# Attention scores with the queries held still: 128 masked query columns, 64 keys passing, four PSUM banks

## The chip, the cores and the metric
The kernel runs on one core of a Trainium2 chip. The metric is the device time of one execution in microseconds. Before the change three runs gave 1270.83, 1270.95 and 1271.89 us, a median of 1270.95 us.

## The reference
Input x has shape (4, 64, 128, 128). Two residual blocks follow each other:
- x is normalised over its 64 channels and cut into windows of 8 x 8 = 64 tokens. q, k and v come from three 64 x 64 projections; there are 4 heads of 16 channels. Each head has scores q k^T / 4 plus a relative position bias (64 x 64 per head), a softmax over the 64 keys, and the product with v. An output projection and the residual x follow.
- Each token is normalised over its channels. A router takes the two best of 8 experts, and their 64 x 64 products are mixed by the renormalised probabilities and added to the token.

All of it is float32 (gates travel as split bfloat16).

## The kernel before
**Tiling.** A strip is 8 rows of one image, 16 windows; there are 16 strips in each of 4 images, 64 in all. On 128 partitions the two halves of the strip lie above each other (`b` = 0 or 1 is the half, in the code also `ab`), so 8 windows lie side by side in two groups `n` of four units `i`; units 0 and 1 are "pair 0", units 2 and 3 "pair 1".

**Stages and slots.** `pipeline` runs slots j = -1 to 66. In slot j a strip is in each of five stages: j+1 is projected and its pair 0 gets scores, j is attended (pair 1, softmax, turning the probabilities), j-1 is put out, j-2 is routed, j-3 is mixed by the experts. Each engine has its order inside a slot written out by hand in its own function `slot`: PE at L533, ACT at L719, DVE at L994, POOL at L1145, SP (which issues all DMAs) at L321. The engines are held together by counting semaphores alone; an engine that waits holds up all that stands behind it in its order. In 24 of the slots (8 for each of images 1 to 3, n = 4 to 11 in `planned`, L242) DVE also sums squares of the next image, `sum_squares` at L815; in 24 (n = 3 to 10) PE also turns input planes, `take` at L352.

**What the change touches.**
- `project` (L365) multiplies the normalised strip by the weights: keys and values first, then, later in the slot, the queries (L571). ACT copies them out of `B_S`: `copy_k` twice (L653; copy e keeps only the heads of parity e by a mask and zeroes the others), `copy_v`, and later `copy_q` once (L648).
- `scores` (L397) makes the scores of one pair: 16 matmuls (2 units, 2 groups n, 2 halves b, 2 head pairs hp), each with 32 contracted rows, a stationary operand of 64 query columns and a moving operand of 128 masked key columns (two head parities by 64 keys). A float32 matmul leaves two matmul and two weight-load records, so a group of scores is 32 records. They lie on four row tiles by two column tiles of the array and all write the two banks of `B_S`. Pair 1 of strip j is the first thing in PE's slot j, pair 0 of strip j+1 comes in the middle (L579).
- `bias` (L878, DVE) adds the position bias and writes `prob` in SBUF; `maxima` (L885, DVE), `shift` (L1117, POOL), `exps` (L673, ACT) and `turn_probs` (L414, PE) follow.
- Between them on DVE stand the gates of the experts: `gate` (L987) for u = 0, 1, 3, 5, 7, and `routing` (L924), small steps in the bank `B_E`. DVE's order in the middle of a slot is: gate 0, gate 1, sum_squares (where there is one), routing steps 1 to 8, gate 3, normalise, bias of pair 0, maxima, gate 5, add_input, gate 7, token_mean.
- PE's order over the same stretch is: expert_biases (L508), gates 0 and 1 (L518), logits, gates 2, turn_logits, gates 3, project queries, experts 0 (L530), turn_probs 2, gates 4, scores of pair 0, take, experts 1, gates 6, turn_probs 3, gates 5, project_out, turn_values, gates 7, experts 2 and 3.

PSUM has eight banks: two for `B_S`, one each for `B_T` (turning), `B_O` (attention output, later its projection), `B_E` (router), `B_P` (sums of probabilities, later odd gates), `B_G` (even gates), `B_Y` (result).

Of the kernel before, what the change touches and what calls it, by code (L numbers as in the profile page):

```python
# [74 lines left out]
def build(nc, x, wqkv, qkvb, kmask, kbias, wproj, wrout, brout, wexp, bexp, bmask, relb, ident, sel, rank, bproj, out):  # L75
    ctx = ExitStack()
    with ctx:
# [3 lines left out]
        def sem(name, per=1, primed=0):  # L81
# [9 lines left out]
        q_bias = sb("q_bias", [P, 1])  # L91
        k_mask = sb("k_mask", [P, 2])
        k_bias = sb("k_bias", [P, 2])
# [9 lines left out]
        rel = sb("rel", [P, HEADS * 2 * NTOK])  # L103
# [18 lines left out]
        q_t = sb("q_t", [P, 2, PAIRS, NTOK])  # L122
        k_m = sb("k_m", [P, 2, PAIRS, 2, NTOK])
# [3 lines left out]
        prob = sb("prob", [P, UNITS, HEADS, 2, NTOK])  # L127
        mx = sb("mx", [P, UNITS, 2 * HEADS])
# [26 lines left out]
        FIRST_SQ = (x_sq, prob[:, 0:2].rearrange("p i h n k -> p (i h n k)").rearrange("p (m c h) -> p m c h", m=2, c=4))  # L155
        B_S = ctx.enter_context(nc.psum_tensor("bank_s", [P, 2, BANK], F32))
        B_T, B_O, B_E, B_P, B_G, B_Y = (
            ctx.enter_context(nc.psum_tensor(f"bank_{n}", [P, BANK], F32)) for n in "toepgy")
        S_S = B_S[:, :, :].rearrange("p g (i e n k) -> p g i e n k", i=2, e=2, n=2)
# [26 lines left out]
        q_ready = sem("q_ready")  # L186
        k_ready = sem("k_ready", 2)
# [47 lines left out]
        consts = [(w_qkv, wqkv), (b_qkv, qkvb), (k_mask, kmask), (k_bias, kbias), (w_proj, wproj), (w_rout, wrout),  # L235
# [112 lines left out]
        def _(pe):  # L348
# [48 lines left out]
            def scores(g, p, pair):  # L397

                if pair == 0:
                    pe.wait_ge(q_ready.sem, q_ready.at(g, 1))  # L400
                    pe.wait_ge(k_ready.sem, k_ready.at(g, 2))
                if not (isinstance(g, int) and g == 0 and pair == 0):
                    pe.wait_ge(s_biased.sem, s_biased.at(g, pair))
                for i in range(2):
                    for n in range(2):
                        for b in range(2):
                            for hp in range(2):
                                rows = slice(C * b + 2 * DH * hp, C * b + 2 * DH * hp + 2 * DH)
                                w = UNITS * n + 2 * pair + i
                                last = mm(S_S[C * b:C * b + C, hp, i, :, n, :], q_t[rows, p, w, :], k_m[rows, p, w, :, :],  # L410
# [3 lines left out]
            def turn_probs(g, i, work):  # L414
# [9 lines left out]
                for h in range(HEADS):  # L424
                    last = tr(B_T[:, h * P:(h + 1) * P], prob[:, i, h].rearrange("p n k -> p (n k)"), idn[:, :])  # L425
                last.then_inc(pt_done.sem, 1)

            def values(g, p):

                pe.wait_ge(pt_ready.sem, pt_ready.at(g, 4))  # L430
                pe.wait_ge(vbd_ready.sem, vbd_ready.at(g, 2))
                pe.wait_ge(x2_ready.sem, x2_ready.at(g))
                for i in range(UNITS):
                    for b in range(2):
                        at = (UNITS * b + i) * NTOK
                        for h in range(HEADS):
                            rows = slice(2 * DH * h, 2 * DH * h + 2 * DH)
                            last = mm(B_O[rows, at:at + NTOK], v_bd[:, p, i, b, h, :],  # L438
                                      prob_t[:, p, i, h, b * NTOK:(b + 1) * NTOK], start=True, stop=True,
# [3 lines left out]
            def prob_sums(g, p):  # L443
# [6 lines left out]
                for i in range(UNITS):  # L450
                    for h in range(HEADS):
                        rows = slice(2 * DH * h, 2 * DH * h + 2 * DH)
                        dst = B_P[rows, :].rearrange("p (b i q) -> p b i q", b=2, i=UNITS)[:, :, i, :]
                        last = mm(dst, ones_bd[:, :], prob_t[:, p, i, h, :].rearrange("p (b q) -> p b q", b=2),  # L454
# [34 lines left out]
            def turn_gates(g):  # L489
                pe.wait_ge(route.sem, route.at(g, route.per))  # L490
                pe.sem_inc(passed, 1)
# [18 lines left out]
            def gates(g, u):  # L510

                if u == 1:
# [20 lines left out]
            def slot(j, p, work, on):  # L533
# [3 lines left out]
                if attending:  # L537
                    scores(j, p, 1)
# [4 lines left out]
                if projecting:  # L543
                    project(j + 1, KEYS_VALUES)
                if outputting:
                    values(j - 1, 1 - p)
                if mixing:
                    residual(j - 3, 1 - p)
                    turn_gates(j - 3)
# [20 lines left out]
                if projecting:  # L570
                    project(j + 1, QUERIES)  # L571
# [6 lines left out]
                if projecting:  # L578
                    scores(j + 1, 1 - p, 0)  # L579
# [8 lines left out]
                if mixing:  # L588
                    gates(j - 3, 5)
# [21 lines left out]
        def _(act):  # L611
# [28 lines left out]
            def first_root(batch):  # L640
# [4 lines left out]
                A(q_bias[:, :], b_qkv[:, 0:1], ACT.Copy, scale=float(DH) ** -0.5).then_inc(set_act.sem, 1)  # L645
                act.wait_ge(set_act.sem, 2)

            def copy_q(g, p):  # L648
# [609 lines left out]
```

## Time and profile before

| | before |
|---|---|
| median of three runs | 1270.95 us |
| profiled execution | 1268.81 us |
| its span, first to last instruction | 1267.0 us |
| PE busy | 1192.4 us, 94% |
| DVE busy | 1053.9 us, 83% |
| ACT busy | 920.4 us, 73% |
| POOL busy | 1081.7 us, 85% |
| mean granted TensorE clock | 0.983 of full speed |

Engines: PE is TensorE's matmuls, PEld its weight loads (they overlap PE), DVE VectorE, ACT ScalarE, POOL GpSimd. A busy PE has a matmul somewhere between start and end; matmuls overlap, so a matmul's own duration says little of its price, and the step from one group's start to the next one's says more. "Idle before, releaser" is time in which an engine waited, with the instruction that ended it.

### The profile page before, as it was taken

The numbers are of one execution on the slowest core, as the hardware profiler recorded it, in microseconds if no ns is written. First come the engines' busy times: TensorE is split into PE (matmuls) and PEld (weight loads), VectorE is DVE, ScalarE is ACT, GpSimd is POOL, SyncE is SP. The second block draws the span as 40 slices with busy tenths as digits, with TensorE's granted clock in tenths as the row PEclk, the third lists the DMA queues.
The fourth block names the chain that finished last, engine by engine and source line by source line (L and its number), as shares of the span: only waits on it lengthen the run. The fifth ranks groups of instructions, "written<-read, shape, count | busy, mean of one in ns | idle before, by whom it ended". The sixth has DMA issues, their size and how long they took to land.

```text
span 1267.0 us, 47630 instructions
## 1 busy us (share of the span) xinstructions
PE 1192.4 (94%) x19840; PEld 729.4 (58%) x19840; DVE 1053.9 (83%) x2247; ACT 920.4 (73%) x1743; POOL 1081.7 (85%) x925
## 2 busy tenths in 40 slices
PE   4579999999999999999999999999999999999986
PEld 3456666655565666656566666655556565666531
DVE  6458898888888889898888888988888888888874
ACT  6368778867777887877677888777767776777742
POOL 6368999989888999999988899998988888888753
PEclk9599999999999999999999999999999999999998
DMA  7012333322223233322222333332222222222221
GB/s 203 5 38 66 92 94 86 81 61 71 55 60 81 77 90 94 91 59 61 70 55 62 95 88 86 88 87 55 58 65 66 53 65 65 63 56 66 64 70 42
DMA packets 95622, 91.43 MB, mean 72 GB/s; under 512 B 26928, under 2 KB 62384, under 8 KB 95408
## 3 DMA queue, kind: packets, MB, share of 16 engines
q1 hardware_dynamic: 95408, 88.37, 27.6%
q8 instruction: 159, 2.61, 0.9%
q14 instruction: 55, 0.45, 0.1%
HBM read 35.90 MB, written 17.83 MB: 42 GB/s over the span
## 4 chain that ended last, share of the span: by engine, by line
PE 67%; DVE 10%; POOL 7%; DMA 7%; issue 5%; ACT 5%; SPq 0%; DVEq 0%; POOLq 0%; ACTq 0%
PE bank_y L530 16%; PE bank_s L410 8%; PE bank_t L425 8%; PE bank_s L384 6%; PE bank_o L464 4%; PE bank_g L518 4%; DMA r_b<-recip_rows 4%; PE bank_o L438 4%; PE bank_p L454 4%; PE bank_p L518 3%; DVE t_g L992 3%; DMA recip_rows<-r_out 2%; PE bank_t L394 2%; PE bank_y L502 2%; DVE prob L880 2%
## 5 line engine op out<-in xcount | busy, mean ns | idle before, releaser
L1142 POOL TENSOR_TENSOR t_g<-t_t,g_copy 128x512 f32<-128x512 f32 x192 | 245.6, 1292 | 72.0 <-ACT g_copy L712 70.8
L530 PE MATMUL bank_y<-t_g,w_exp 128*64 128x512 f32 x1024 | 268.9, 616 | 6.7 <-DVE t_g L992 4.7
L1120 POOL TENSOR_TENSOR prob<-prob,mx 128x512 f32<-128x512 f32 x256 | 261.8, 1045 | 14.7 <-DVE mx L887 14.5
L675 ACT ACTIVATE prob<-prob 128x512 f32<-128x512 f32 x256 | 159.4, 623 | 128.6 <-POOL prob L1120 128.6
L992 DVE TENSOR_TENSOR t_g<-t_t,bank_p 128x512 f32<-128x512 f32 x256 | 174.2, 680 | 9.2 <-PE bank_p L518 7.3
L880 DVE TENSOR_TENSOR prob<-bank_s,rel 128x1024 f32<-128x1024 f32 x128 | 156.3, 1221 | 28.4 <-PE bank_s L410 23.7
L425 PE MATMUL bank_t<-idn,prob 128*128 128x128 f32 x1024 | 163.6, 283 | 5.5 <-ACT v_bd L670 5.0
L679 ACT ACTIVATE prob_t<-bank_t 128x512 f32<-128x512 f32 x256 | 152.5, 596 | 21.3 <-PE bank_t L425 21.2
L712 ACT ACTIVATE g_copy<-bank_g 128x512 f32<-128x512 f32 x192 | 113.8, 593 | 74.1 <-PE bank_g L518 73.9
L425 PEld LDWEIGHTS bank_t<-idn,prob 128*128 128x128 f32 x1024 | 112.8, 141 | 79.2 <-issue 65.9
L887 DVE TENSOR_REDUCE mx<-prob 128x16 f32<-128x1024 f32 x128 | 155.4, 1214 | 2.2
L410 PEld LDWEIGHTS bank_s<-k_m,q_t 32*64 32x64 f32 x4096 | 112.5, 134 | 71.5 <-issue 69.2
L410 PE MATMUL bank_s<-k_m,q_t 32*64 32x128 f32 x4096 | 143.8, 277 | 1.5 <-ACT q_t L650 1.1
L1132 POOL TENSOR_TENSOR ln<-ln,mhalf 128x8 f32<-128x8 f32 x64 | 105.5, 1648 | 38.5 <-DVE ln L919 38.3
L384 PE MATMUL bank_s<-xn,w_qkv 64*64 64x128 f32 x3072 | 115.7, 281 | 18.5 <-DVE xn L874 13.6
L384 PEld LDWEIGHTS bank_s<-xn,w_qkv 64*64 64x64 f32 x3072 | 84.4, 135 | 45.9 <-issue 45.8
L530 PEld LDWEIGHTS bank_y<-t_g,w_exp 128*64 128x64 f32 x1024 | 53.3, 135 | 95.5 <-issue 78.8
L518 PE MATMUL bank_g<-g_t,gate_sel 128*128 128x512 bf16 x256 | 98.6, 385 | 5.1 <-DVE t_g L992 1.8
L518 PE MATMUL bank_p<-g_t,gate_sel 128*128 128x512 bf16 x256 | 98.2, 383 | 4.2 <-DVE t_g L992 3.6
L1103 POOL TENSOR_TENSOR x_b<-xt,b_proj 128x512 f32<-128x512 f32 x64 | 100.0, 1562 | 0.0
L992 DVE TENSOR_TENSOR t_g<-t_t,bank_g 128x512 f32<-128x512 f32 x64 | 44.0, 688 | 66.7 <-PE bank_g L518 66.7
L655 ACT ACTIVATE k_m<-bank_s,k_bias,k_mask 128x512 f32<-128x512 f32 x128 | 92.7, 775 | 7.7 <-PE bank_s L384 7.6
(122 smaller groups left out, 2345.1 us busy)
## 6 DMA issues: line engine op xcount, KB each, us to landing
t_t<-t_rout SPq DMA_DIRECT2D x256, 128.0 KB, 2.4
x_in<-in_x SPq DMA_DIRECT2D x68, 256.0 KB, 3.3
r_b<-recip_rows SPq DMA_DIRECT2D x64, 256.0 KB
out_y<-y_out SPq DMA_DIRECT2D x128, 128.0 KB, 2.6
r_in<-sum_b SPq DMA_DIRECT2D x64, 16.0 KB
recip_rows<-r_out SPq DMA_DIRECT2D x64, 16.0 KB, 1.7
t_g<-in_sel SPq DMA_DIRECT2D x1, 512.0 KB, 3.6
rel<-in_relb SPq DMA_DIRECT2D x1, 256.0 KB, 2.9
```

What stands on the lines that cost most here:

```text
L384: last = mm(dst[:, n], w_qkv[rows, i, :], src[:, n, ab], start=True, stop=True, skip_group_check=True)
L410: last = mm(S_S[C * b:C * b + C, hp, i, :, n, :], q_t[rows, p, w, :], k_m[rows, p, w, :, :], start=True, stop=True, skip_group_check=True)
L425: last = tr(B_T[:, h * P:(h + 1) * P], prob[:, i, h].rearrange("p n k -> p (n k)"), idn[:, :])
L518: mm(B_GATE[u % 2][:, :], gate_sel16[:, u, :], g_t[:, :], start=True, stop=True).then_inc(gate_done[u % 2].sem, 1)
L530: mm(B_Y[C * a:C * a + C, :], w_exp[:, pair, :], t_g[:, (2 * pair + a) % TG, :], start=False, stop=(pair == MIXES // 2 - 1), skip_group_ch ...
L675: A(prob[:, i], prob[:, i], ACT.Exp).then_inc(p_ready.sem, 1)
L679: A(prob_t[:, p, i].rearrange("p h q -> p (h q)"), B_T[:, :], ACT.Copy).then_inc(pt_ready.sem, 1)
L880: V.tensor_tensor(prob[:, 2 * pair:2 * pair + 2].rearrange("p i (g e) n k -> p g i (e n k)", e=2), B_S[:, :, :].rearrange("p g (i s) -> p ...
L887: V.tensor_reduce(mx[:, 2 * pair:2 * pair + 2, :].rearrange("p i s -> p (i s)"), prob[:, 2 * pair:2 * pair + 2].rearrange("p i h n k -> p ...
L992: V.tensor_tensor(t_g[:, u % TG, :], t_t[:, p, u % 2, :], B_GATE[u % 2][:, :], ALU.mult).then_inc(tg_dve.sem, 1)
L1120: G.tensor_tensor(sc, sc, mx[:, i, :].unsqueeze(2).broadcast_to([P, 2 * HEADS, NTOK]), ALU.subtract).then_inc(s_shifted.sem, 1)
L1142: G.tensor_tensor(t_g[:, u % TG, :], t_t[:, p, u % 2, :], g_copy[:, n, :], ALU.mult).then_inc(tg_pool.sem, 1)
```

## The change
Queries and keys swap their parts.
- q is now copied twice, masked by head parity (`q_mask` holds the scale 1/4 in the kept rows), and k once, plain. `project` makes queries and values first and the keys at the later place.
- A scores matmul has a stationary operand of 128 columns (parity by 64 queries) and 64 moving key columns. There are still 16 in a group. The array now has four row tiles and no column tiles, and each row tile (2b + hp) writes a bank of its own.
- For this the eight banks get fixed numbers. Pair 0 writes the upper halves of `B_P`, `B_E` and the two banks of `B_S`; pair 1 writes the lower halves of the two banks of `B_S`, of `B_G` and of `B_O`. The router's scratch moves to the lower half of `B_E`.
- New waits on PE. Scores of pair 0: for the copied sums, for routing step 8 of strip j-2, and for DVE's gate 3 of strip j-3. Scores of pair 1: for add_input and the last gate copy of the slot before. `values`, `turn_gates`: for the bias of pair 1. `gates` 5: for the bias of pair 0.
- Layouts of `prob`, `mx` and the bias table follow; `shift` now reads and writes 4 x 2 x 64 elements with a gap between the 4, and `exps` 4 pieces of 128.

The orders of all engines' slots are otherwise as they were.

```diff
+        BANKS = ctx.enter_context(nc.psum_tensor("banks", [P, 8, BANK], F32))
+        B_P, B_E, B_G, B_O, B_T, B_Y = (BANKS[:, n, :] for n in (0, 1, 4, 5, 6, 7))
+        B_S = BANKS[:, 2:4, :]
+        S_S = (BANKS[:, 0:4, BANK // 2:BANK], BANKS[:, 2:6, 0:BANK // 2])
...
             def project(g, parts):
-                if parts == QUERIES:
-                    pe.wait_ge(k_ready.sem, k_ready.at(g, 2))
+                if parts == KEYS:
+                    pe.wait_ge(q_ready.sem, q_ready.at(g, 2))
...
-            def scores(g, p, pair):
+            def scores(g, p, pair, on):
+                projecting, attending, outputting, routing_on, mixing = stages(on)
                 if pair == 0:
-                    pe.wait_ge(q_ready.sem, q_ready.at(g, 1))
-                    pe.wait_ge(k_ready.sem, k_ready.at(g, 2))
+                    pe.wait_ge(q_ready.sem, q_ready.at(g, 2))
+                    pe.wait_ge(k_ready.sem, k_ready.at(g, 1))
+                    if outputting:
+                        pe.wait_ge(sum_copied.sem, sum_copied.at(g - 1))
+                    if routing_on:
+                        pe.wait_ge(route.sem, route.at(g - 3, 8))
+                    if mixing:
+                        pe.wait_ge(tg_dve.sem, tg_dve.at(g - 4, ON_DVE.index(3) + 1))
+                else:
+                    if outputting:
+                        pe.wait_ge(x2_ready.sem, x2_ready.at(g - 1))
+                    if g >= 4:
+                        pe.wait_ge(g_copied.sem, g_copied.at(g - 3))
...
-                                last = mm(S_S[C * b:C * b + C, hp, i, :, n, :], q_t[rows, p, w, :], k_m[rows, p, w, :, :],
+                                at = (2 * i + n) * NTOK
+                                last = mm(S_S[pair][:, 2 * b + hp, at:at + NTOK],
+                                          q_m[rows, p, w, :, :].rearrange("p e q -> p (e q)"), k_t[rows, p, w, :],
...
             def values(g, p, attending):
+                if attending:
+                    pe.wait_ge(s_biased.sem, s_biased.at(g + 1, 2))
...
             def turn_gates(g, attending):
                 pe.wait_ge(route.sem, route.at(g, route.per))
+                if attending:
+                    pe.wait_ge(s_biased.sem, s_biased.at(g + 3, 2))
...
             def gates(g, u, projecting=False):
+                if u == 5 and projecting:
+                    pe.wait_ge(s_biased.sem, s_biased.at(g + 4, 1))
...
             def shift(g, i):
-                sc = prob[:, i].rearrange("p h n k -> p (h n) k")
-                G.tensor_tensor(sc, sc, mx[:, i, :].unsqueeze(2).broadcast_to([P, 2 * HEADS, NTOK]),
+                sc = prob[:, i // 2, :, i % 2]
+                G.tensor_tensor(sc, sc, mx[:, i // 2, :, i % 2].unsqueeze(3).broadcast_to([P, HEADS, 2, NTOK]),
...
-KEYS_VALUES, QUERIES = (1, 2), (0,)
+QUERIES_VALUES, KEYS = (0, 2), (1,)
```

## Rows read from the trace of the kernel before
**Rows 1.** The page: busy time of PE, and the chain that ended last.
```profile
PE 1192.4 (94%) x19840; PEld 729.4 (58%) x19840; DVE 1053.9 (83%) x2247; ACT 920.4 (73%) x1743; POOL 1081.7 (85%) x925
...
PE 67%; DVE 10%; POOL 7%; DMA 7%; issue 5%; ACT 5%; SPq 0%; DVEq 0%; POOLq 0%; ACTq 0%
```
**Rows 2.** Timeline of PE, a slot with sum_squares and take: start, length, line.
```profile
473.02 0.38 PE L518 MATMUL bank_g<-g_t,gate_sel 128*128 128x512 bf16 x1
...
477.59 1.10 PE L410 MATMUL bank_s<-k_m,q_t 32*64 32x128 f32 x32
478.62 0.65 PE L362 MATMUL bank_t<-idn,x_in 128*128 128x128 f32 x4
...
480.99 0.38 PE L518 MATMUL bank_p<-g_t,gate_sel 128*128 128x512 bf16 x1
...
491.74 0.38 PE L518 MATMUL bank_g<-g_t,gate_sel 128*128 128x512 bf16 x1
```
**Rows 3.** Timeline of DVE in the same slot.
```profile
474.64 1.98 DVE L819 TENSOR_REDUCE sums<-x_sq 128x128 f32<-128x1024 f32 x1
...
478.49 0.68 DVE L992 TENSOR_TENSOR t_g<-t_t,bank_p 128x512 f32<-128x512 f32 x1
479.09 0.68 DVE L900 TENSOR_TENSOR o_t<-bank_o,r_b 128x512 f32<-128x512 f32 x1
```
**Rows 4.** Timelines of PE, then DVE, a slot without sum_squares.
```profile
604.01 0.38 PE L518 MATMUL bank_g<-g_t,gate_sel 128*128 128x512 bf16 x1
...
608.50 1.10 PE L410 MATMUL bank_s<-k_m,q_t 32*64 32x128 f32 x32
...
611.21 0.38 PE L518 MATMUL bank_p<-g_t,gate_sel 128*128 128x512 bf16 x1
...
607.79 0.68 DVE L992 TENSOR_TENSOR t_g<-t_t,bank_p 128x512 f32<-128x512 f32 x1
...
609.67 1.22 DVE L880 TENSOR_TENSOR prob<-bank_s,rel 128x1024 f32<-128x1024 f32 x1 [0.60 <-PE bank_s L410]
```
**Rows 5.** Slices of 20 ns, L410 alone: its matmuls and loads in flight.
```profile
615.36:615.38 0.02, 0.02 (x4) 0.02 (x4) 1.00 0.00 0
...
615.42:615.44 0.02, 0.02 (x4) 0.02 (x8) 1.00 0.00 0
...
615.50:615.52 0.02, 0.02 (x5) 0.02 (x5) 1.00 0.00 0
...
615.64:615.66 0.02, 0.02 (x12) 0.02 (x8) 1.00 0.00 0
...
616.08:616.10 0.02, 0.02 (x12) 0.02 (x8) 1.00 0.00 0
```
**Rows 6.** Groups by line and form: busy us, mean ns of one, idle before.
```profile
L410 PEld LDWEIGHTS bank_s<-k_m,q_t 32*64 32x64 f32 x4096 | 112.5, 134 | 71.5 <-issue 69.2 <-ACT q_t L650 2.2
...
L464 PE MATMUL bank_o<-w_proj,o_t 128*64 128x64 f32 x2048 | 74.6, 227 | 3.0 <-DVE o_t L900 3.0
...
L454 PEld LDWEIGHTS bank_p<-prob_t,ones_bd 128*32 128x32 f32 x2048 | 52.0, 109 | 11.6 <-issue 11.6
```
**Rows 7.** The same view: the transposes' loads, the squares, and two POOL operations.
```profile
L1120 POOL TENSOR_TENSOR prob<-prob,mx 128x512 f32<-128x512 f32 x256 | 261.8, 1045 | 14.7 <-DVE mx L887 14.5
...
L425 PEld LDWEIGHTS bank_t<-idn,prob 128*128 128x128 f32 x1024 | 112.8, 141 | 79.2 <-issue 65.9 <-ACT prob L675 8.5
...
L1103 POOL TENSOR_TENSOR x_b<-xt,b_proj 128x512 f32<-128x512 f32 x64 | 100.0, 1562 | 0.0
...
L819 DVE TENSOR_REDUCE sums<-x_sq 128x128 f32<-128x1024 f32 x28 | 55.4, 1977 | 7.9 <-ACT x_sq L628 7.9
```
**Rows 8.** Timelines of PE, then DVE: sum_squares without take, every eighth such slot.
```profile
552.39 1.10 PE L410 MATMUL bank_s<-k_m,q_t 32*64 32x128 f32 x32
554.20 1.08 PE L530 MATMUL bank_y<-t_g,w_exp 128*64 128x512 f32 x4 [0.70 <-DVE t_g L992]
...
553.37 0.68 DVE L992 TENSOR_TENSOR t_g<-t_t,bank_p 128x512 f32<-128x512 f32 x1
```

More of the change, by code:

```diff
@@ L72, in at, with build @@
         return n * self.per + (k + self.primed)
-def build(nc, x, wqkv, qkvb, kmask, kbias, wproj, wrout, brout, wexp, bexp, bmask, relb, ident, sel, rank, bproj, out):
+def build(nc, x, wqkv, qkvb, qmask, qbias, wproj, wrout, brout, wexp, bexp, bmask, relb, ident, sel, rank, bproj, out):
     ctx = ExitStack()
@@ L424, in turn_probs, with values @@
                 for h in range(HEADS):
-                    last = tr(B_T[:, h * P:(h + 1) * P], prob[:, i, h].rearrange("p n k -> p (n k)"), idn[:, :])
+                    last = tr(B_T[:, h * P:(h + 1) * P], prob[:, i // 2, h, i % 2].rearrange("p n k -> p (n k)"), idn[:, :])
                 last.then_inc(pt_done.sem, 1)
-            def values(g, p):
+            def values(g, p, attending):
+                if attending:
+                    pe.wait_ge(s_biased.sem, s_biased.at(g + 1, 2))
                 pe.wait_ge(pt_ready.sem, pt_ready.at(g, 4))
@@ L537, in slot @@
                 if attending:
-                    scores(j, p, 1)
+                    scores(j, p, 1, on)
                 if outputting:
@@ L543, in slot @@
                 if projecting:
-                    project(j + 1, KEYS_VALUES)
+                    project(j + 1, QUERIES_VALUES)
                 if outputting:
-                    values(j - 1, 1 - p)
+                    values(j - 1, 1 - p, attending)
                 if mixing:
                     residual(j - 3, 1 - p)
-                    turn_gates(j - 3)
+                    turn_gates(j - 3, attending)
                 if work.take:
@@ L570, in slot @@
                 if projecting:
-                    project(j + 1, QUERIES)
+                    project(j + 1, KEYS)
                 if mixing:
@@ L578, in slot @@
                 if projecting:
-                    scores(j + 1, 1 - p, 0)
+                    scores(j + 1, 1 - p, 0, on)
                 if work.take:
@@ L588, in slot @@
                 if mixing:
-                    gates(j - 3, 5)
+                    gates(j - 3, 5, projecting)
                 if outputting:
@@ L674, in exps @@
                 act.wait_ge(s_shifted.sem, s_shifted.at(g, i + 1))
-                A(prob[:, i], prob[:, i], ACT.Exp).then_inc(p_ready.sem, 1)
+                unit = prob[:, i // 2, :, i % 2].rearrange("p h n k -> p h (n k)")
+                A(unit, unit, ACT.Exp).then_inc(p_ready.sem, 1)
             def copy_probs(g, p, i):
@@ L924, in routing @@
             def routing(g, first_step, last_step):
-                lead, hot, rest, gates = (
-                    B_E[:, n * ROUTE_AT:(n + 1) * ROUTE_AT].rearrange("p (r e) -> p r e", e=EXPERTS) for n in range(2, 6))
+                hot, rest, lead, gates = (
+                    B_E[:, n * ROUTE_AT:(n + 1) * ROUTE_AT].rearrange("p (r e) -> p r e", e=EXPERTS) for n in range(4))
                 lg = B_E[:, 0:P].rearrange("p (k x) -> p k x", x=ROUT)[:, :, 0:2 * EXPERTS].rearrange("p k (a e) -> p k a e", a=2)
```

87 lines of the change are left out of this document (42 added, 45 removed).

## The prediction
> **What bounds the kernel now.** I read the page first: PE is busy 94% of the span, and the chain that ended last lies on PE for 67% of it [rows 1]. Then the timelines of single slots, because an average says nothing about which engine closes the loop. In a slot with sum_squares and take, gates 0 starts at 473.02 and again at 491.74: 18.72 us a slot, with no idle time noted on PE in between [rows 2]. DVE works beside it. What the reader is to see in [rows 2, 3] is how two engines meet in the middle of a slot. DVE's gate 3 ends at 478.49 + 0.68 = 479.17, 6.15 us after PE started gates 0, because sum_squares (1.98) stands before it. PE starts the scores of pair 0 at 477.59, 4.57 us after gates 0, and waits for none of that. In a slot without sum_squares the same two points nearly coincide: gate 3 ends at 607.79 + 0.68 = 608.47, the scores start at 608.50 [rows 4].
>
> **Part 1: the score matmuls.** A group holds 32 matmul records and takes 1.03 us of PE (477.59 to 478.62) [rows 2]. The slices show its rhythm. Four loads are in flight at once in the first slice. Four more have joined 0.06 us later, and the first four are all but gone at 615.50, together. Then the count of loads peaks at 615.64 and again, four rounds on, at 616.08 [rows 5]. So four row tiles load and multiply side by side, in eight rounds of about 0.44 / 4 = 0.11 us; I use 107 ns, so that 8 x 0.107 = 0.86 us, and the other 0.17 of 1.03 is the change-over at the group's ends, which I leave as it is. A round is as long as the slower of its two halves: passing 128 columns, or loading 64.
>
> After the change 64 columns pass and 128 are loaded. Passing costs no more than half, 53 ns. What a 128-column load costs here no row shows; its bounds are these. From above: L464 loads 64 columns and passes 64, on two column tiles. Its 2048 records keep PE busy 74.6 us in 64 groups of 32 [rows 6], 1.17 us a group of 16 rounds. Of L410's 1.10 [rows 2], 0.86 are rounds and 0.24 the two ends; with the same ends a round of L464 is (1.17 - 0.24) / 16 = 58 ns. So 64 columns load in at most 58 and 128 in at most 116. From below: nothing excludes 53 ns, the passing time, since the 128-column loads of the transposes have records of 141 ns against 134 for 64 columns [rows 6, 7]. Which is nearer? The loads of the same kind (float32 matmuls) go from 109 ns for 32 columns to 134 for 64 [rows 6], 25 ns for 32 columns or 0.78 ns a column; 128 columns are then 100 ns. The transposes are another mode. So I take the round at 107 ns: **the scores cost what they cost before, saving 0** (from below: 8 x 0.054 = 0.43 us saved a group, two groups a slot).
>
> The Trainium skill, in "TensorE: Matmul & The Clock Gate", section "LDWEIGHTS (loading the stationary operand)", puts a load at its columns divided by 1.2 ns, whatever the rows. An estimate from that page is 107 ns for 128 columns and 53 for 64; no run here shows the first.
>
> **Part 2: the new wait of pair 0.** scores(j+1, 0) now waits for DVE's gate 3 of strip j-3; routing step 8 stands before it on DVE, so gate 3 is the one that ends last. From DVE's end to PE's start I take 0.10 us ([rows 8]: DVE ends at 554.05, the waiting L530 starts at 554.20, 0.15; a bound below is none).
> - Slot with sum_squares and take: 479.17 + 0.10 = 479.27 in place of 477.59, **+1.68 us**. Behind it on PE stand take, experts 1, gates 6, turn_probs 3, gates 5, project_out, turn_values, gates 7 and experts 2 and 3, and then the next slot down to its gates 0. DVE's gates 5 and 7 and add_input wait for these and move too; the next gate 3 comes a fixed 6.15 us after the next gates 0. So nothing takes the 1.68 back. L819 has 28 records; 4 are before the slots, 24 in them [rows 7], and 3 of those have no take. 21 x 1.68 = 35.3 us.
> - sum_squares without take: gate 3 ends at 554.05, so the scores start at 554.15 in place of 552.39, +1.76. But experts 1 already waited 0.70 for the same gate [rows 8], and that wait goes: +1.06, x 3 = 3.2 us.
> - The other slots in which strips are both projected and mixed (j = 3 to 61 are 59, less 24: 35): 608.57 in place of 608.50 [rows 4], +0.07, x 35 = 2.5 us.
>
> **Part 3: what I cost at nothing.** gates 5 now waits for the bias of pair 0. The bias starts 1.17 us after the scores (608.50 to 609.67) and takes 1.22 [rows 4]; in the long slot it would end at 479.27 + 2.39 = 481.66, and PE reaches gates 5 at 480.99 + 1.68 = 482.67 [rows 2]. In the short slot it ends at 608.57 + 2.39 = 610.96 against 611.28. Covered by 1.0 and 0.3 us; without that cover project_out and add_input would be late. values and turn_gates wait for the bias of pair 1, but project, which stands before both, waits for it already. Pair 1's waits point at work of the slot before that DVE and ACT leave behind well ahead of its end. The copies on ACT are three in either version, and the one that the scores need is now the plain keys at the old place, before the new wait ends. The bias, maxima and router steps handle the same number of elements. The bias table is half as large, loaded while statistics are made.
>
> **Sum.** 35.3 + 3.2 + 2.5 = 41 us. The profiled execution took 1268.81 us and would take 1310; the median of the runs stands 2.1 us above it, so against it the sum gives 1270.95 + 41 = 1312. I say **1311 us**.
>
> **Rivals.**
> - **A, the load is short and hidden** (ends on the other side). Place: the rounds of L410. Price: with 53 ns a round the two groups give back 0.86 us of PE a slot. Long slots: 1.68 - 0.86 = +0.82, x 21 = +17; the three without take +0.2 each. Short slots: PE alone would give 0.07 - 0.86 = -0.79, but DVE then sets the pace. Its bias had waited 0.60 [rows 4]; with the scores starting 0.07 later and 0.43 shorter, it starts 0.36 earlier, and only that is sure. So -0.36 to -0.79, x 35 = -13 to -28. Net +5 to -10, middle -2: 1269 us, range 1260 to 1277. It decides by s, what a group saves: if the short slots keep all but the 0.07, 59 x 2s must exceed the 41, so s over 0.35, a round under 63 ns; if they keep only 0.36, even s = 0.43 leaves +5. For it: the 141 ns of the transposes' loads [rows 7]. Against: the slope of the matmuls' own loads. The Trainium skill, in the same page's section "The mechanism" of its part on packing small matmuls, has row tiles loading and multiplying side by side and the pass alone setting the time. By that rule the time would be this rival's; [rows 5] agree on the side-by-side part, and no row on a load longer than its pass.
> - **B, loads follow each other with a gap.** If a load can't begin until the one before is taken over, a round is longer: the second four loads stand 0.06 to 0.08 us behind the first [rows 5], some 22 ns more than 53, so 107 + 22 = 129 ns, 8 x 0.022 = 0.18 us a group. 59 slots x 0.36 = +21: 1332 us. L464, where load and pass match, shows no such gap.
> - **C, POOL's shift is dearer.** Its operand now has a gap between four pieces: 1045 ns as it is, 1562 for L1103, POOL's dearest operation with strides of this size [rows 7]. Two shifts stand before centre_tokens, on the way to the next slot's tokens: up to 2 x 0.52 = 1.03 us a slot, half of it over 59 slots is +30: 1341 us. For nothing dearer: the inner run of 64 and the broadcast stay.
>
> **How the numbers follow.** Forecast (round 107, wait paid) 0.55, its own range 1300 to 1320 (lag 0 to 0.15, a round 5 ns either way). A 0.28, B 0.10, C 0.07. The range 1263 to 1335 takes in the forecast, B, and most of A; it leaves out A's lower end (0.07) and most of C with B's upper end (0.1). About 0.2% is what this measurement can tell from no change. Faster by more: over half of A, 0.16. Within 0.2%: 0.06. Slower: 0.78.
>
> **What would show it.** Right: in slots with sum_squares PE idle about 1.7 us before L410's middle group, released by DVE's L992; a group of scores still 1.03 us apart from the next; load records of L410 at 180 to 190 ns (134 + 50), matmul records near 221. Slots without squares unchanged. A: load records near 141, a group at 0.6 us. B: a group at 1.2. C: L1120 above 1.1 us. The prediction is wrong if the wait is there and the total isn't longer.

## The result, and the profile after

| | before, on the same chip | after |
|---|---|---|
| median | 1271.42 us (1270.83 to 1272.45) | 1328.62 us (1327.58 to 1336.58) |
| ratio | | 1.0465, interval 1.0429 to 1.05 |
| profiled execution | 1268.81 us | 1329.49 us |
| its span | 1267.0 us | 1327.7 us |
| mean granted TensorE clock | 0.983 | 0.967 |

The kernel became 57 us slower; the prediction had 41. The page of the changed kernel, busy time and the chain that ended last (all PSUM tiles are now called "banks"):

```profile
PE 1196.1 (90%) x19715; PEld 753.6 (57%) x19840; DVE 1065.3 (80%) x2247; ACT 926.8 (70%) x1743; POOL 1085.1 (82%) x925
...
PE 69%; DVE 14%; issue 5%; POOL 2%; DMA 2%; ACT 1%; SPq 0%; DVEq 0%; POOLq 0%
```

PE is busy for only 4 us more than in [rows 1] and DVE for 11, while the span grew by 60.7. The 4 is too low by some 13: 125 matmul records are missing from the new trace (19715 for 19840), one of gates in each of 62 slots, whose place shows as an idle 0.16 (L537 has 450 matmul records and 512 of loads), and 63 of expert_biases. Even so the new time is mostly time in which PE stands still, and DVE's share of the last chain rose from 10 to 14%. The chain's shares alone would not have told where. The groups of instructions do (busy us, mean ns of one | idle before and its releasers):

```profile
L1141 POOL TENSOR_TENSOR prob<-prob,mx 128x512 f32<-128x512 f32 x256 | 263.0, 1049 | 13.9 <-DVE mx L908 13.9
...
L421 PE MATMUL banks<-k_t,q_m 32*128 32x64 f32 x4096 | 148.6, 282 | 53.2 <-DVE t_g L1013 49.4 <-DVE x L929 1.2 <-ACT k_t L675 0.9
L421 PEld LDWEIGHTS banks<-k_t,q_m 32*128 32x128 f32 x4096 | 132.6, 192 | 125.9 <-issue 124.1 <-DVE x L929 1.8
```

Three readings, and one row of before for the first. The scores (L421, before L410) waited 49.4 us for DVE's gates at L1013. The same group of the kernel before:

```profile
L410 PE MATMUL bank_s<-k_m,q_t 32*64 32x128 f32 x4096 | 143.8, 277 | 1.5 <-ACT q_t L650 1.1 <-DVE prob L880 0.5
```

There PE had stood still for 1.5 us in all ahead of the scores, and for none of DVE's gates. The load record of 128 columns is 192 ns, 58 more than the 134 of 64 columns. And POOL's shift costs 1049 ns, against 1045 in [rows 7]: the gap between its four pieces costs nothing.

A slot with sum_squares and take, the counterpart of [rows 2]; timeline of PE (start, length, line):

```profile
505.91 0.38 PE L537 MATMUL banks<-g_t,gate_sel 128*128 128x512 bf16 x1
508.06 1.12 PE L421 MATMUL banks<-k_t,q_m 32*128 32x64 f32 x32 [1.78 <-DVE t_g L1013]
509.11 0.66 PE L361 MATMUL banks<-idn,x_in 128*128 128x128 f32 x4
509.70 1.08 PE L549 MATMUL banks<-t_g,w_exp 128*64 128x512 f32 x4
...
511.37 0.38 PE L537 MATMUL banks<-g_t,gate_sel 128*128 128x512 bf16 x1
...
515.52 1.12 PE L421 MATMUL banks<-k_t,q_m 32*128 32x64 f32 x32
```

and DVE beside it, the counterpart of [rows 3]:

```profile
503.27 1.99 DVE L840 TENSOR_REDUCE sums<-x_sq 128x128 f32<-128x1024 f32 x1
...
507.13 0.68 DVE L1013 TENSOR_TENSOR t_g<-t_t,banks 128x512 f32<-128x512 f32 x1
...
509.24 1.23 DVE L901 TENSOR_TENSOR prob<-banks,rel 128x1024 f32<-128x1024 f32 x1 [0.83 <-PE banks L421]
```

PE has finished gates 4 and stands for 1.78 us until gate 3 ends on DVE at 507.13 + 0.68 = 507.81. The scores start at 508.06, 0.25 after it. The group itself takes 508.06 to 509.11 = 1.05 us, where it took 1.03. The period from one middle group to the next (508.06 to 528.57) is 20.51 us, where a slot took 18.72.

A slot without sum_squares, PE and then DVE, the counterpart of [rows 4]:

```profile
1014.83 1.12 PE L421 MATMUL banks<-k_t,q_m 32*128 32x64 f32 x32 [0.18 <-DVE t_g L1013]
...
1013.89 0.68 DVE L1013 TENSOR_TENSOR t_g<-t_t,banks 128x512 f32<-128x512 f32 x1
```

Gate 3 ends at 1014.57, the scores start 0.26 later: the same step from DVE's end to PE's start, here only 0.18 of it idle. The same slot in the kernel before, PE and then DVE:

```profile
959.98 1.10 PE L410 MATMUL bank_s<-k_m,q_t 32*64 32x128 f32 x32
...
959.37 0.68 DVE L992 TENSOR_TENSOR t_g<-t_t,bank_p 128x512 f32<-128x512 f32 x1
```

There the scores had started 0.07 us before gate 3 ended (959.37 + 0.68 = 960.05). Of the 34 slots without squares of the table below, 25 are like this one; only 6 are like the slot of [rows 4], where the scores start 0.03 after it.

**Where the 57 us lie.** I set the starts of DVE's bias of pair 1, one a slot, against those of the kernel before. The length of a slot from one such start to the next then gives the growth of each slot:

| stretch | growth, sum | typical slot |
|---|---|---|
| 24 slots with sum_squares | +47.1 us | +1.78; four of them +2.8 to +3.4 |
| 34 slots without | +7.0 us, 0.2 on average | two kinds: 16 of them +0.25 to +0.45, 13 under +0.1 |
| ahead of these slots | +2.9 us | |

Together 57.0. The two profiled executions lie 60.7 us apart; the other 3.7 are behind the last of these slots, and the medians lie 57.2 apart. The four slots that stand out and the two ends of the kernel are dealt with below, under the clock.

### The profile page after: what moved, and what is told of

Its sections match the earlier page's. It is cut to its first block, busy times and chain, and to the rows that moved or that the text cites. A ratio compares the mean times of both kernels' runs of the same rounds, so it can differ in the third digit from the quotient of the medians.

```text
span 1327.7 us, 47813 instructions
## 1 busy us (share of the span) xinstructions
PE 1196.1 (90%) x19715; PEld 753.6 (57%) x19840; DVE 1065.3 (80%) x2247; ACT 926.8 (70%) x1743; POOL 1085.1 (82%) x925
## 4 chain that ended last, share of the span: by engine, by line
PE 69%; DVE 14%; issue 5%; POOL 2%; DMA 2%; ACT 1%; SPq 0%; DVEq 0%; POOLq 0%
PE banks L549 16%; PE banks L421 9%; PE banks L437 7%; PE banks L537 6%; PE banks L383 6%; PE banks L479 5%; DVE t_g L1013 5%; PE banks L452 4%; PE banks L469 4%; DVE sums L840 3%; PE banks L393 3%; PE banks L519 2%; PE banks L489 2%; PE banks L361 2%; DMA r_b<-recip_rows 1%
## 5 line engine op out<-in xcount | busy, mean ns | idle before, releaser
L1013 DVE TENSOR_TENSOR t_g<-t_t,banks 128x512 f32<-128x512 f32 x320 | 213.2, 683 | 89.9 <-PE banks L537 82.8
L549 PE MATMUL banks<-t_g,w_exp 128*64 128x512 f32 x1024 | 273.0, 626 | 3.6 <-DVE t_g L1013 2.8
L1141 POOL TENSOR_TENSOR prob<-prob,mx 128x512 f32<-128x512 f32 x256 | 263.0, 1049 | 13.9 <-DVE mx L908 13.9
L421 PEld LDWEIGHTS banks<-k_t,q_m 32*128 32x128 f32 x4096 | 132.6, 192 | 125.9 <-issue 124.1
L901 DVE TENSOR_TENSOR prob<-banks,rel 128x1024 f32<-128x1024 f32 x128 | 156.6, 1224 | 57.8 <-PE banks L421 51.7
L421 PE MATMUL banks<-k_t,q_m 32*128 32x64 f32 x4096 | 148.6, 282 | 53.2 <-DVE t_g L1013 49.4
L437 PE MATMUL banks<-idn,prob 128*128 128x128 f32 x1024 | 166.5, 286 | 12.9 <-issue 10.3
L537 PE MATMUL banks<-g_t,gate_sel 128*128 128x512 bf16 x450 | 162.5, 389 | 16.8 <-DVE t_g L1013 7.6
L700 ACT ACTIVATE prob_t<-banks 128x512 f32<-128x512 f32 x256 | 152.5, 596 | 25.8 <-PE banks L437 24.9
L437 PEld LDWEIGHTS banks<-idn,prob 128*128 128x128 f32 x1024 | 115.0, 143 | 76.6 <-issue 59.3
L1153 POOL TENSOR_TENSOR ln<-ln,mhalf 128x8 f32<-128x8 f32 x64 | 105.5, 1648 | 47.2 <-DVE ln L940 47.2
L383 PE MATMUL banks<-xn,w_qkv 64*64 64x128 f32 x3072 | 117.4, 284 | 17.7 <-DVE xn L895 13.7
L537 PEld LDWEIGHTS banks<-g_t,gate_sel 128*128 128x128 bf16 x512 | 50.0, 98 | 95.7 <-issue 58.6
```

The lines of the kernel that those rows point to most:

```text
L383: last = mm(dst[:, n], w_qkv[rows, i, :], src[:, n, ab], start=True, stop=True, skip_group_check=True)
L421: last = mm(S_S[pair][:, 2 * b + hp, at:at + NTOK], q_m[rows, p, w, :, :].rearrange("p e q -> p (e q)"), k_t[rows, p, w, :], start=True, s ...
L437: last = tr(B_T[:, h * P:(h + 1) * P], prob[:, i // 2, h, i % 2].rearrange("p n k -> p (n k)"), idn[:, :])
L537: mm(B_GATE[u % 2][:, :], gate_sel16[:, u, :], g_t[:, :], start=True, stop=True).then_inc(gate_done[u % 2].sem, 1)
L549: mm(B_Y[C * a:C * a + C, :], w_exp[:, pair, :], t_g[:, (2 * pair + a) % TG, :], start=False, stop=(pair == MIXES // 2 - 1), skip_group_ch ...
L700: A(prob_t[:, p, i].rearrange("p h q -> p (h q)"), B_T[:, :], ACT.Copy).then_inc(pt_ready.sem, 1)
```

## The experiments

The question was whether the wait for gate 3 is the whole of it, what a 128-column load really costs, and what either would be without the other. The kernel before, run beside these, had medians of 1270.97 us (e1, e2, e4, e5), 1271.41 us (e3, e6, e7, e8) and 1272.09 us (e9, e10).

### e1: the wait alone, in the kernel before

```diff
-            def scores(g, p, pair):
+            def scores(g, p, pair, mixing=False):
...
                     pe.wait_ge(k_ready.sem, k_ready.at(g, 2))
+                    if mixing:
+                        pe.wait_ge(tg_dve.sem, tg_dve.at(g - 4, ON_DVE.index(3) + 1))
```

> The kernel before with one line more: the scores of pair 0 wait for DVE's gate 3 of strip j-3, which they need not here. Theory W (the wait is what the change costs): in the 24 slots with sum_squares PE idles 1.7 to 1.8 us before the scores, in the others 0.1 to 0.2, and the granted clock falls after some of these idles, as in the changed kernel; 24 x 1.75 + 35 x 0.15 + some 8 of slow clock gives 1315 to 1328 us. Rival F (the new form of the scores, its banks and layouts cost a good part): under 1300 us.

Measured: 1321.18 us, ratio 1.0391 (1.0371 to 1.041). One wait, with nothing else changed, costs 50 of the 57 us. PE's timeline of e1 in a long slot:

```profile
479.67 1.10 PE L412 MATMUL bank_s<-k_m,q_t 32*64 32x128 f32 x32 [1.79 <-DVE t_g L994]
480.70 0.66 PE L362 MATMUL bank_t<-idn,x_in 128*128 128x128 f32 x4
```

The idle time is that of the changed kernel to within 0.01 us, and the group is still 1.03 us. In e1 the 24 long slots grew by 39.7 us (1.73 typically, none stands out) and the 34 short ones by 7.3. So the short slots' growth belongs to the wait too. What e1 does not have is 7.4 us of the long slots, and 2.6 ahead of them. One part of its expectation failed: the granted clock was to fall after some of these idle times, and it fell after none of the 24.

### e7: all the new waits, in the kernel before

```diff
+                    if outputting:
+                        pe.wait_ge(sum_copied.sem, sum_copied.at(g - 1))
+                    if routing_on:
+                        pe.wait_ge(route.sem, route.at(g - 3, 8))
+                    if mixing:
+                        pe.wait_ge(tg_dve.sem, tg_dve.at(g - 4, ON_DVE.index(3) + 1))
+                else:
+                    if outputting:
+                        pe.wait_ge(x2_ready.sem, x2_ready.at(g - 1))
+                    if g >= 4:
+                        pe.wait_ge(g_copied.sem, g_copied.at(g - 3))
...
+                if u == 5 and projecting:
+                    pe.wait_ge(s_biased.sem, s_biased.at(g + 4, 1))
```

(and the waits of `values` and `turn_gates`, as in the change.)

> The kernel before with all the new waits of the changed kernel, not only the one for gate 3, and its old scores, banks and layouts. Theory W: only the wait for gate 3 has a price, so this takes what the kernel with that wait alone took (1321.2 us), within 3 us. Rival: the waits for the biases, the input sum or the gate copies cost too, and this comes to the changed kernel's 1328 us or above.

Measured: 1319.58 us, ratio 1.0374 (1.0354 to 1.0393). That is no more than e1's 1321.18. PE's waits for gate 3 (us in total, times, longest), in the table of waits of e1, then of e7:

```profile
PE bank_s L412 <- DVE t_g L994: 51.0, 54, 1.9
```

```profile
PE bank_s L421 <- DVE t_g L1009: 51.6, 56, 1.9
```

The other seven waits are covered, as Part 3 of the prediction had them. This is also the measure of e1's and e7's own error: two kernels that do the same differ by 1.6 us.

### e2: the changed kernel with sum_squares moved ahead

`sum_squares` moves on DVE from behind gate 1 to in front of gate 0, right behind the reciprocals, so that it no longer stands between gates 0 and gate 3.

```diff
                 if outputting:
                     reciprocals(j - 1)
+                if work.sums:
+                    sum_squares(work.batch, *work.sums)
...
-                if work.sums:
-                    sum_squares(work.batch, *work.sums)
```

> The changed kernel with DVE's sum_squares ahead of gate 0, where DVE idled 1.1 us, instead of between gate 1 and the routing steps. Theory W: gate 3 then comes about 5.0 us after gates 0 instead of 6.15, the wait falls from 1.78 to about 0.5 us in 24 slots (-27 to -31), and with idles that short the clock does not fall (-8): 1288 to 1298 us. Rival F: the wait was not what cost, over 1318 us.

Measured: 1293.98 us, ratio 1.0181 (1.0166 to 1.0196). 35 of the 57 us come back by moving one DVE instruction, the 6 us of the clock (below) among them. Timeline of e2, a long slot, PE and then DVE:

```profile
490.96 1.12 PE L421 MATMUL banks<-k_t,q_m 32*128 32x64 f32 x32
...
485.01 1.87 DVE L840 TENSOR_REDUCE sums<-x_sq 128x128 f32<-128x1024 f32 x1
...
490.03 0.68 DVE L1013 TENSOR_TENSOR t_g<-t_t,banks 128x512 f32<-128x512 f32 x1
```

Gate 3 ends at 490.71, the scores start 0.25 later with no idle time noted. The 24 long slots grew by 13.1 us, 0.54 typically, instead of 47.1. What is left has a new place, since gate 0 now waits behind the squares and PE's later gates behind it. The waits of PE's loads for DVE's gates in the changed kernel, and then in e2:

```profile
PEld banks L537 <- DVE t_g L1013: 22.0, 48, 1.3
```

```profile
PEld banks L537 <- DVE t_g L1013: 42.4, 94, 1.3
```

### e3: the same move in the kernel before

The edit is that of e2, made in the kernel before.

> The kernel before with DVE's sum_squares ahead of gate 0. A control for the same move in the changed kernel: there it took 35 us off. Theory W: here no score waits for gate 3, so nothing is to be gained; gates 2 on PE wait for DVE's gate 0, which comes 0.9 us later, so 24 slots lose up to 0.5 us: 1271 to 1283 us. Rival (sum_squares in that place is bad for any version): under 1265 us.

Measured: 1280.83 us, ratio 1.0068 (1.0053 to 1.0084). Here the move costs 9 us: 7.9 of them in the long slots, 0.39 typically. So sum_squares stood in the right place before, when nothing on PE waited for gate 3, and stands in the wrong one once the scores do. It also says what the change costs if both kernels have the new order: 1293.98 against 1280.83, 13 us; against the kernel before as it was it is 23.

### e4: 64 columns held instead of 128

Of the 128 query columns only the first 64 are held still from strip 2 on; the scores of the other parity's heads are left out there.

```diff
-                                last = mm(S_S[pair][:, 2 * b + hp, at:at + NTOK],
-                                          q_m[rows, p, w, :, :].rearrange("p e q -> p (e q)"), k_t[rows, p, w, :],
+                                held = q_m[rows, p, w, :, :].rearrange("p e q -> p (e q)")
+                                cols = P if g < 2 else P // 2
+                                last = mm(S_S[pair][0:cols, 2 * b + hp, at:at + NTOK], held[:, 0:cols], k_t[rows, p, w, :],
```

> The changed kernel, but from the third strip on only the first 64 query columns (one head parity) are held still; the scores of the other two heads are not computed. 64 columns loaded, 64 passing, the same four row tiles and banks. Theory L (a round is as long as its load): the load record falls from 192 to about 134 ns, the round from 107 to about 54, a group of scores from 1.05 to 0.60 to 0.65 us; the time falls to 1280 to 1295 us. Rival P (the round is set by something that row tiles share, not by the columns loaded): a group stays at 1.05 us and the time at 1325 to 1330.

Measured: 1307.03 us, ratio 1.0283 (1.0249 to 1.0316), above what was expected. Timeline of e4 (PE) in a long slot:

```profile
499.33 0.69 PE L423 MATMUL banks<-k_t,q_m 32*64 32x64 f32 x32 [1.81 <-DVE t_g L1014]
499.96 0.66 PE L361 MATMUL banks<-idn,x_in 128*128 128x128 f32 x4
```

and its loads, in the groups of instructions:

```profile
L423 PEld LDWEIGHTS banks<-k_t,q_m 32*64 32x64 f32 x3968 | 72.9, 136 | 126.6 <-issue 124.8 <-DVE x L930 1.8
```

The part on the load came out: the group falls from 1.05 to 0.63 us, and with the pass unchanged at 64 columns only the load can have held it up. (1.05 - 0.63) / 8 = 53 ns a round, which is 64 columns' worth. What failed is the step from there to the time. The 124 groups of strips 2 to 63 save 0.42 x 124 = 52 us on PE; 1328.62 - 1307.03 = 22 arrive. By the same table as above, each of the 34 short slots keeps 0.33 of the 0.84 on average, 11 us in all; that DVE then sets the pace there is my reading, no run shows it. In long slots the typical growth falls from 1.78 only to 1.15, and in ten of the 24 the clock fell, which cost each about 1.6 (below): 16 us, where the full change lost 6. The 24 long slots together save only 6.3.

### e5: 32 keys passing instead of 64

Here only 32 of the 64 keys pass from strip 2 on, and the scores of the other 32 are left out. The load stays at 128.

```diff
+                                keys = NTOK if g < 2 else NTOK // 2
+                                last = mm(S_S[pair][:, 2 * b + hp, at:at + keys], held, k_t[rows, p, w, 0:keys],
```

> The changed kernel, but from the third strip on only 32 of the 64 keys pass each matmul; the scores of the other half of the keys are not computed. 128 columns loaded, 32 passing. Theory L: the load sets the round, so a group of scores stays at 1.02 to 1.05 us and the time within 0.5% of 1328. A rival in which load and pass add up (107 = 53 + 53): the round falls to about 80 ns, a group to 0.83 us, and the time by 15 us or more.

Measured: 1337.91 us, ratio 1.0518 (1.0489 to 1.0548): slower than the full change by 0.7%, where no difference was expected. Timeline of e5 (PE):

```profile
494.52 1.09 PE L423 MATMUL banks<-k_t,q_m 32*128 32x32 f32 x32 [1.78 <-DVE t_g L1014]
495.55 0.66 PE L361 MATMUL banks<-idn,x_in 128*128 128x128 f32 x4
```

and in the groups of instructions:

```profile
L423 PEld LDWEIGHTS banks<-k_t,q_m 32*128 32x128 f32 x4096 | 134.2, 194 | 126.2 <-issue 124.8 <-DVE x L930 1.4
```

Halving the pass takes 0.02 us from the group (1.03 for 1.05); halving the load took 0.42. That settles which half sets the round; load and pass added up, the other possibility that the expectation named, would have given 0.83. The total missed its 0.5%. In the profiled run, 1332.07 us and still within it, five long slots stand out by 1.6 to 3.1 us at half clock. The other three runs took 1338 to 1341 us at a lower mean granted clock (0.957 to 0.961 for 0.970); they have no trace, so that the clock is the cause there too is likely and not shown.

The pair also decides between two readings of the load. The Trainium skill, in "TensorE: Matmul & The Clock Gate", section "LDWEIGHTS (loading the stationary operand)", gives columns / 1.2 ns, 107 ns for 128: the traces agree, since 64 columns fewer save 53 ns a round (e4), and e5's 1.03 us is eight rounds of 107 with the 0.17 of the prediction for the group's ends. By the Trainium skill's section "The mechanism", in the same page's part on packing small matmuls, row tiles run side by side and the pass sets the time; e5 disagrees, since there the pass is a quarter of the load and the group is as long as before.

### e9 and e10: is anything to be had from a short group?

e9 is the changed kernel with e4's half load and e2's move together. e10 is the kernel before with one of two head parities passing (64 columns instead of 128, load 64 as it was), so the scores of the other parity are left out:

```diff
+                                par = slice(0, 2 if g < 2 else 1)
-                                last = mm(S_S[C * b:C * b + C, hp, i, :, n, :], q_t[rows, p, w, :], k_m[rows, p, w, :, :],
+                                last = mm(S_S[C * b:C * b + C, hp, i, par, n, :], q_t[rows, p, w, :], k_m[rows, p, w, par, :],
```

> The changed kernel with both moves: 64 query columns held (the scores of one head parity are not computed from the third strip on) and sum_squares ahead of gate 0. It asks whether the changed form would have paid with a cheap load and a short wait. From 1294.0 (sum_squares first, full load), 0.43 us less a group: if PE alone sets the pace, 2 x 0.43 x 59 = -51, 1243 us; if the long slots' wait for gate 3 and DVE's chain hold the rest back as in the run with half the load alone (where 22 of 51 us came), 1265 to 1275 us.

> The kernel before with only one head parity of 64 masked keys passing from the third strip on (the scores of the other parity are not computed): 64 columns loaded, 64 passing, none of the new waits. Theory L: rounds of 54 ns, a group of 0.60 to 0.65 us. How much of the 51 us that PE saves arrives? If PE alone sets the pace: 1220 us. If DVE's chain (gate 3, bias, variance, then POOL's two steps to the tokens) has as little slack as the timelines show, 0.05 us in a long slot and 0.3 to 0.6 in a short one: 1248 to 1262 us.

Measured: e9 1263.72 us, ratio 0.994 (0.9919 to 0.9962); e10 1255.32 us, ratio 0.9876 (0.986 to 0.9892). Timeline of e10 (PE), a long slot:

```profile
492.90 0.69 PE L411 MATMUL bank_s<-k_m,q_t 32*64 32x64 f32 x32
493.54 0.65 PE L362 MATMUL bank_t<-idn,x_in 128*128 128x128 f32 x4
494.67 1.08 PE L531 MATMUL bank_y<-t_g,w_exp 128*64 128x512 f32 x4 [0.49 <-DVE t_g L993]
```

The group is 0.64 us, 0.39 shorter, and the very next instruction that needs gate 3 gives it back: experts 1 waits 0.49 for DVE, where the kernel before shows no idle time ahead of it in such a slot. Of 0.39 x 124 = 48 us on PE, 17 reach the end. So even a score matmul at half its price is worth only 1.2% in this kernel. I take that as about what the change could have brought with a hidden load and without its wait; no run has just that. e9, with the wait shortened, has 8 us and comes out just below its expectation's case in which the wait and DVE's chain hold the rest back (1265 to 1275), far from the one of PE alone (1243).

### e6 and e8: shortening PE's order in the kernel before

Looking for a version that beats both, I put `values` right behind `prob_sums` (e6), so that the array keeps 32-column tiles over both; e8 moves turn_probs 0 behind `project` as well.

```diff
                 if outputting:
                     prob_sums(j - 1, 1 - p)
+                    values(j - 1, 1 - p)
...
-                if outputting:
-                    values(j - 1, 1 - p)
```

> The kernel before with PE's values moved right behind prob_sums, both on column tiles of 32. If the 0.17 us at the ends of a group is the array's change from one tiling to another, one change less a slot saves 0.10 to 0.17 us in 61 slots: 1261 to 1266 us. If it is a group's own fill and drain, nothing: 1270 to 1272 us.

> As the one before it, and turn_probs 0 moved behind project, beside the other full-array transposes (ACT's copy of it moved behind the second key copy): two changes of tiling less a slot. If changes cost: 1251 to 1262 us, unless the keys' and values' copies, now ahead of the copy of the probabilities, hold up turn_probs 1; then no better than the one before it.

Measured: e6 1304.16 us, ratio 1.0257 (1.0235 to 1.028); e8 1307.62 us, ratio 1.0276 (1.0259 to 1.0293). e6 misses both of its cases, and e8 its first; the second, no better than e6, is what came. Timeline of e6, PE and then ACT:

```profile
648.20 1.08 PE L454 MATMUL bank_p<-prob_t,ones_bd 128*32 128x128 f32 x32
649.10 1.08 PE L438 MATMUL bank_o<-prob_t,v_bd 128*32 128x64 f32 x64
650.10 0.66 PE L425 MATMUL bank_t<-idn,prob 128*128 128x128 f32 x4
...
654.65 0.38 PE L518 MATMUL bank_g<-g_t,gate_sel 128*128 128x512 bf16 x1 [0.93 <-ACT g_t L707]
...
650.79 0.60 ACT L678 ACTIVATE prob_t<-bank_t 128x512 f32<-128x512 f32 x1 [0.85 <-PE bank_t L425]
```

The saving is there: from prob_sums to values it is 0.90 us, against 1.01 from prob_sums to its next neighbour in the changed kernel (516.57 to 517.58) and in the kernel before, 0.11 less, and no change of tiling between the two. But turn_probs 0 now comes about 1 us later, ACT stands 0.85 for it, and everything behind on ACT moves, down to the copy of the gates (g_t), for which PE then waits 0.93. The 0.1 was bought with 0.9: that is what the fastest of the short slots grew by (from 17.94 us), and the long ones grew by 0.3. e8 has the same 0.90 us from prob_sums to values, but its next turning waits as long:

```profile
656.91 0.63 PE L425 MATMUL bank_t<-idn,prob 128*128 128x128 f32 x4 [0.90 <-ACT prob_t L678]
```

That is turn_probs 1, waiting for ACT to copy what turn_probs 0 made, behind both copies of the keys: the very condition that the expectation had named. No version was found that computes everything and beats the kernel before.

## The clock, and the slots that stand out

The growth of e1's slots is even; the changed kernel's is not. Here is what a slot that grew by over 2.8 us looks like, in its timeline of PE:

```profile
445.02 1.12 PE L421 MATMUL banks<-k_t,q_m 32*128 32x64 f32 x32 [1.76 <-DVE t_g L1013]
446.07 1.12 PE L361 MATMUL banks<-idn,x_in 128*128 128x128 f32 x4
447.12 1.98 PE L549 MATMUL banks<-t_g,w_exp 128*64 128x512 f32 x4
```

take and experts 1 last almost twice as long as in the fence of 508.06 (1.12 for 0.66, 1.98 for 1.08). Stretches of 2 us of the same kernel (length, PE busy and its matmuls, granted clock, DMA):

```profile
442.00:444.00 2.00, 1.26 (x9) 1.00 0.08 31
444.00:446.00 2.00, 0.98 (x32) 1.00 0.77 177
446.00:448.00 2.00, 2.00 (x13) 0.51 0.81 201
448.00:450.00 2.00, 1.67 (x9) 0.63 0.49 147
450.00:452.00 2.00, 2.00 (x39) 1.00 0.00 0
```

and of e1 in the same slot, whose scores start there at 438.60:

```profile
440.00:442.00 2.00, 2.00 (x13) 1.00 0.77 205
```

Behind an idle 1.76 us and one group of scores the granted clock falls from full speed, 2.4 GHz, to half, 1.2 GHz, for under 4 us, which costs that slot 1.55. It happens in 4 of 24 long slots: 6.2 us. In the other three the clock falls between 0.5 and 2.2 us after the scores have started. At the start the return to full speed is later too; the first 80 us of the changed kernel have

```profile
40.00:60.00 20.00, 13.84 (x172) 0.50 0.00 1
60.00:80.00 20.00, 16.80 (x310) 0.74 0.06 17
```

where the kernel before was granted 0.59 and 0.89. This is the place of the 2.9 us ahead of the slots, but that the clock is their cause is not shown. e6 was granted full speed there,

```profile
40.00:60.00 20.00, 14.12 (x177) 1.00 0.00 1
```

and still reached the slots 0.4 us later than the kernel before. Behind the slots, the last 64 us had a granted clock of 0.86 where the kernel before had 0.94. e1 has the same 0.86 and the same 3.6 us there, e2 has 0.95 and only 0.4. So these 3.7 us go with the clock, as far as the profiles show.

How often the clock fell in the 24 long slots, in the one profile of each: e1 0 and e7 1; the full change 4; e5 5; e4 10; and e2, where PE does not stand still ahead of the scores, 0. In the short slots of these runs it never fell. So each fall had an idle time of about 1.8 us ahead of it, and most such idle times had none behind them. e1 and e7 do the same work and differ by one, which says how rough these counts are. The runs do not show why one slot falls and its equal neighbour does not, nor why e4 has so many. I leave that open.

## Why the prediction came out as it did

**Right: the direction, the mechanism and its place.** The forecast case was "round 107, wait paid". The wait stands where it was put, before the middle group, released by gate 3, in every long slot, and e1 shows it alone to be worth 50 us.

Point by point, by the prediction's own steps:

- **Part 1, scores save 0.** The group is 1.05 us where it was 1.03, the load record 192 ns where 180 to 190 was named. The matmuls' own load slope (0.78 ns a column, [rows 6]) was the right neighbour, and the transposes' 141 ns [rows 7] the wrong one. The rounds, in slices of 20 ns of L421 alone:

```profile
508.34:508.36 0.02, 0.02 (x12) 0.02 (x7) 1.00 1.51 411
...
508.46:508.48 0.02, 0.02 (x12) 0.02 (x8) 1.00 0.00 0
...
508.56:508.58 0.02, 0.02 (x12) 0.02 (x7) 1.00 0.47 102
...
508.68:508.70 0.02, 0.02 (x12) 0.02 (x8) 1.00 0.90 205
```

The count of matmuls peaks every (508.68 - 508.34) / 3 = 0.11 us, the rhythm of [rows 5], though half as many columns pass. The 0.02 that the group grew by was not foreseen.
- **Part 2, long slots, 21 x 1.68.** Measured 1.78 typically, and this is the term that the runs of e1, e2 and e7 bear out. The chain of the working held: gate 3 still ends 6.16 us after gates 0 (501.65 to 507.81), nothing took the time back. The term that was mis-sized is the lag from DVE's end to PE's start, taken as 0.10 from the 0.15 of [rows 8] and in truth 0.25; e1, with the old form of the scores, has 0.26, so the new form is not what makes it. The full account of the 1.78: 1.68, + 0.15 of lag, + 2 x 0.02 of the two groups, - 0.10, because take to experts 1 is 0.59 us in the new trace where the same step was 0.69 before, so experts 1 had been waiting a little for gate 3 already. That is 1.77.
- **Slots with squares and no take, 3 x 1.06.** The two of them without a fall of the clock grew by 1.22 and 1.26 (e1: 1.15), which is the same lag again.
- **Short slots, 35 x 0.07 = 2.5 us.** Measured 7.0 us in 34. Two things were wrong. The lag is one: 0.25 for 0.10. The other is the slot of [rows 4], which is not a typical one. Where the scores had started 0.08 before gate 3 ended, the new start is 0.25 + 0.08 = 0.33 later, and with 0.04 for the two groups the fastest such slots went from 17.94 to 18.31 us. Others were longer already and hardly grew. A small number taken 59 times over is no small number; the range for the forecast reached only to 0.15.
- **Part 3, nothing.** e7 confirms it for the waits. gates 5 is reached 0.90 us after the bias has ended (511.37 against 509.24 + 1.23), where 1.0 was worked out.
- **The clock: missed.** No term of the sum and no rival allowed for it, though PE was to stand still 1.7 us in 24 slots. It costs 6.2 us in four slots, and the 3.7 behind the last slots go with it. The 2.9 at the start are not explained.

In sum, over the stretches of the table. Long slots: 38.5 predicted (35.3 + 3.2), + 24 x 0.15 = 3.6 of lag, - 21 x 0.10 = 2.1 that experts 1 had waited before, + 24 x 0.04 = 1.0 of the groups, + 6.2 of the clock: 47.2, measured 47.1. Short slots: 34 x 0.07 = 2.4 predicted, + 34 x 0.15 = 5.1 of lag: 7.5, measured 7.0. That these two agree is luck, since the slots are of two kinds and neither grew by 0.2. At the start 2.9, predicted none. The result of 1328.6 lies in the range of 1263 to 1335 and outside the forecast's own 1300 to 1320, whose ends allowed for the lag up to 0.15 and for no clock.

**The rivals.** A (the load is hidden) is refuted by the group of 1.05 us and by e4 beside e5. Even where a group is made as short by halving the load, the time is 1307, not 1269. So A's own price was too low as well. It had the wait in it, but the long slots of e4 grew by 1.15 where it had 0.82, the short ones came out 0.12 shorter on average where it had 0.36 to 0.79, and the clock took 16 us. B (a gap between loads, round 129 ns, group 1.2) is refuted by the same 1.05; its 1332 us lies nearer the result than the forecast, by luck. C (POOL's shift dearer) is refuted by 1049 ns.

## What to carry to other kernels

When operands are swapped, compare the longer of load and pass before and after, not their sum: four row tiles side by side don't hide a load of 128 columns behind a pass of 64, and 128 by 64 costs what 64 by 128 did. A wait for a buffer is priced by what stands ahead of its releaser on the releaser's own engine. Here that was a 2 us reduction, free in the kernel before because the scores did not wait behind it; look for such an instruction first, since moving it returned 35 of 57 us. Count the slots of each kind before one slot's number is multiplied: here the slot that was read stood for 6 of 34. And where an order leaves PE idle for a microsecond or two at a regular place, allow for a clock that may fall behind it.

## What was not expected of the hardware

- A float32 load of 128 columns for a 32-row tile leaves a record of 192 ns, while the transposes' float32 load of 128 columns leaves one of 143 in the same trace. The record of one kind of matmul was no guide to the other.
- The granted clock falls to half within 0.5 to 2.2 us of the scores' start behind an idle time of 1.76 to 1.84 us, in 4 of 24 slots and not in the others, and then costs 1.6 us.
- From DVE's end to the start of a waiting PE group lie 0.25 us in the score groups, where one such step in [rows 8] was 0.15.
- The group of prob_sums is followed after 0.90 us by a group of the same tiling (e6, e8) and after 1.01 by one of another. Only this pair of groups was tried; that the change of tiling costs the 0.11 us is the likely reading, not a shown one.
